# Selective scan on one core: dt replication ahead of the y products, and dt and du released step by step

## The reference, cut to what matters

```python
def step(h, inp):
    u_t, dt_t, B_t, C_t = inp
    dA = jnp.exp(jnp.clip(dt_t[..., None] * A, -20.0, 0.0))
    dB_u = jnp.clip(dt_t[..., None] * B_t[:, None, :] * u_t[..., None], -10.0, 10.0)
    h = jnp.clip(h * dA + dB_u, -100.0, 100.0)
    y = jnp.einsum('bds,bs->bd', h, C_t)
    return (h, y)
h0 = jnp.zeros((Bsz, d_inner, d_state), u.dtype)
_, ys = jax.lax.scan(step, h0, xs)      # one step for each of the T tokens
```

## Time and profile before

| | |
|---|---|
| median of three runs | 6533.08 us |
| profiled execution, its own time | 6532.31 us |
| its span, first to last instruction | 6530.6 us |
| the scan's part of it (first dt matmul at 4350.1, last y product at 5867.7) | 1517.6 us |
| VectorE busy over the span | 4930.3 us (75%) |
| ScalarE busy over the span | 3779.0 us (58%) |

### The profile page before, as it was taken

How to read it: one execution, slowest core, us unless ns; L and a number is a source line. 1 busy time by engine, 2 the same in 40 slices (tenths; PEclk the granted TensorE clock), 3 DMA queues, 4 the chain that set the end, 5 groups by cost and what they waited for, 6 DMA issues and landing times. The chain is left out here.

```text
span 6530.6 us, 93690 instructions
## 1 busy us (share of the span) xinstructions
PE 5225.0 (80%) x27420; PEld 2029.7 (31%) x27420; DVE 4930.3 (75%) x10471; ACT 3779.0 (58%) x5329; POOL 1363.7 (21%) x1658
## 2 busy tenths in 40 slices
PE   6979799797979799795999644438888888877778
PEld 3333333333333333333666322201111111115555
DVE  6666675767666675766888698879999999986768
ACT  4555555555555555552444466657777777774433
POOL 0000000000000000000111244443333333334421
PEclk8989899897989899897999866655555555558999
DMA  0000000000000000001111133331111111115422
GB/s 23 1 14 1 14 1 1 14 1 14 1 14 1 14 1 1 7 1 38 42 41 42 61 117 117 111 106 44 45 45 45 44 44 45 45 39 161 156 90 71
DMA packets 198904, 273.56 MB, mean 42 GB/s; under 512 B 13989, under 2 KB 157989, under 8 KB 192454
## 3 DMA queue, kind: packets, MB, share of 16 engines
q1 hardware_dynamic: 181190, 252.90, 12.7%
q10 hardware_dynamic: 17408, 16.78, 0.7%
HBM read 151.14 MB, written 118.49 MB: 41 GB/s over the span
## 5 line engine op out<-in xcount | busy, mean ns | idle before, releaser
L644 DVE TENSOR_REDUCE at_nmax<-at_ps_t 128x1 f32<-128x512 f32 x2048 | 1321.1, 686 | 584.4 <-PE at_ps_t L344 567.1
L486 ACT ACTIVATE at_probsT<-at_ps_s 128x1024 f32<-128x1024 f32 x1024 | 1046.0, 1023 | 810.3 <-PE at_ps_s L369 810.3
L2045 DVE SCALAR_TENSOR_TENSOR sc_decayed<-sc_da,sc_state 128x256 f32<-128x256 f32 x2048 | 777.3, 425 | 141.5 <-ACT sc_da L2000 141.5
L2000 ACT ACTIVATE sc_da<-sc_da,sc_a_col 128x1024 f32<-128x1024 f32 x512 | 560.0, 1094 | 346.2 <-PE sc_da L1936 346.2
L2055 DVE CUSTOM_DVE_ANT_0 sc_state<-sc_xd,sc_decayed 128x256 f32<-128x256 f32 x2048 | 757.3, 410 | 0.0
L344 PE MATMUL at_ps_t<-at_qkT 108*128 108x512 bf16 x2048 | 711.5, 413 | 42.8 <-DVE at_nmax L644 19.4
L1912 POOL TENSOR_SCALAR sc_xd<-sc_xd 128x1024 f32<-128x1024 f32 x512 | 533.1, 1041 | 957.4 <-ACT sc_xd L2007 957.4
L1948 PE MATMUL sc_ps_du<-sc_parts,sc_sel 24*128 24x512 bf16 x1024 | 565.4, 609 | 203.5 <-ACT sc_xd L2007 203.5
L2007 ACT ACTIVATE sc_xd<-sc_ps_du,sc_bt 128x512 f32<-128x512 f32 x1024 | 651.8, 696 | 5.9 <-PE sc_ps_du L1948 5.9
L378 PE MATMUL at_ps_o<-at_probsT,at_v 128*32 128x256 f32 x8192 | 633.2, 392 | 1.2
L365 PE MATMUL at_ps_s<-at_qkT 108*128 108x512 bf16 x2048 | 624.0, 387 | 0.0
(11 more groups left out here) (308 smaller groups left out, 7983.5 us busy)
## 6 DMA issues: line engine op xcount, KB each, us to landing
dt_parts<-si_pt SPq DMA_DIRECT2D x64, 384.0 KB, 2.6
du_parts<-si_pu SPq DMA_DIRECT2D x64, 384.0 KB, 3.2
sc_parts<-dt_parts SPq DMA_DIRECT2D x128, 192.0 KB
sc_parts<-du_parts SPq DMA_DIRECT2D x128, 192.0 KB
u_tok<-si_ut SPq DMA_DIRECT2D x8, 2048.0 KB, 8.3
y<-sc_yo SPq DMA_DIRECT2D x256, 64.0 KB
so_yin<-y SPq DMA_DIRECT2D x32, 512.0 KB
so_uin<-u_tok SPq DMA_DIRECT2D x32, 512.0 KB
```

Source lines behind the costliest of these rows:

```text
L486: nc.scalar.activation(probsT[:, c % RING, :], ps_s[c % 2][:], ACT.Exp).then_inc(s_exp, 1)
L644: nc.vector.tensor_reduce(nmax[:, par, c, t:t + 1], ps_t[c][:], AX_X, ALU.max, negate=True).then_inc(s_max, 1)
L2000: nc.scalar.activation(flat, flat, ACT.Exp, scale=a_col[:]).then_inc(s_da, 1)
L2045: nc.vector.scalar_tensor_tensor(decayed[:, ch], da[q % 2][:, j % 2, ch], DECAY_MIN, state[:, (j - 1) % SRING, ch], ALU.max, ALU.mult).the ...
```

## The change

It has four parts. In TensorE's turn dt of pair q + 2 now stands ahead of the y products of the last round, where it stood behind them. Each dt matmul waits only for its own step of the pair that held the buffer before, instead of both waiting for the whole pair. Each dt and du matmul counts its semaphore up by one, where only the second of a pair did. And ScalarE's `inputs` waits before each of its two copies for that step's du, where it waited once for both. `decays` still waits for both steps, and SyncE waits for the same matmuls under the new count.

```diff
--- before.py
+++ after.py
@@ -1855,8 +1855,8 @@
             def turn(it, g, first, last):
                 for h in range(2):
                     if not last:
-                        sp.wait_ge(s_rdt, it * NPAIR + h * HP + HP)
-                        sp.wait_ge(s_rdu, it * NPAIR + h * HP + HP)
+                        sp.wait_ge(s_rdt, it * STEPS + (h + 1) * TL)
+                        sp.wait_ge(s_rdu, it * STEPS + (h + 1) * TL)
                         load(it + 1, h)
                     if h == 0 and not first:
                         store(it - 1, 1 - g)
@@ -1930,12 +1930,11 @@
                 h = q // HP
                 if q % HP == 0:
                     pe.wait_ge(s_in[h][0], 16 * it + 16)
-                if not first:
-                    pe.wait_ge(s_dec, (n - 1) * 2 * NC)
                 for j in range(2):
-                    last = nc.tensor.matmul(da[q % 2][:, j], sel[0:KR, :], parts[0:KR, h, q % HP * 2 + j],
-                                            start=True, stop=True)
-                last.then_inc(s_rdt, 1)
+                    if not first:
+                        pe.wait_ge(s_dec, ((n - LEAD) * 2 + j + 1) * NC)
+                    nc.tensor.matmul(da[q % 2][:, j], sel[0:KR, :], parts[0:KR, h, q % HP * 2 + j],
+                                     start=True, stop=True).then_inc(s_rdt, 1)
 
             def replicate_du(it, q, first=False):
                 n = it * NPAIR + q
@@ -1945,9 +1944,9 @@
                 for j in range(2):
                     if not (first and q == 0):
                         pe.wait_ge(s_xd, 2 * n - 1 + j)
-                    last = nc.tensor.matmul(ps_du[:, j * HALF:(j + 1) * HALF], sel[Q1:Q1 + KR, :],
-                                            parts[Q1:Q1 + KR, h, q % HP * 2 + j], start=True, stop=True)
-                last.then_inc(s_rdu, 1)
+                    nc.tensor.matmul(ps_du[:, j * HALF:(j + 1) * HALF], sel[Q1:Q1 + KR, :],
+                                     parts[Q1:Q1 + KR, h, q % HP * 2 + j], start=True, stop=True
+                                     ).then_inc(s_rdu, 1)
 
             def add_y(it, g, r):
                 if r == 0:
@@ -1962,14 +1961,14 @@
 
             def turn(it, g, first, last):
                 for q in range(NPAIR):
+                    if q + LEAD < NPAIR:
+                        replicate_dt(it, q + LEAD)
+                    elif not last:
+                        replicate_dt(it + 1, q + LEAD - NPAIR)
                     if q % 2 == 0 and q > 0:
                         add_y(it, g, q // 2 - 1)
                     elif q == 0 and not first:
                         add_y(it - 1, 1 - g, ROUNDS - 1)
-                    if q + LEAD < NPAIR:
-                        replicate_dt(it, q + LEAD)
-                    elif not last:
-                        replicate_dt(it + 1, q + LEAD - NPAIR)
                     if q + LEAD + 1 < NPAIR:
                         replicate_du(it, q + LEAD + 1)
                     elif not last:
@@ -1995,15 +1994,15 @@
                 nc.scalar.copy(yo[:, g], ps_y[:]).then_inc(s_yo, 1)
 
             def decays(n, q):
-                act.wait_ge(s_rdt, n + 1)
+                act.wait_ge(s_rdt, 2 * n + 2)
                 flat = da[q % 2][:].rearrange("p j d -> p (j d)")
                 nc.scalar.activation(flat, flat, ACT.Exp, scale=a_col[:]).then_inc(s_da, 1)
 
             def inputs(n, q, fresh=False):
-                act.wait_ge(s_rdu, n + 1)
                 if not fresh:
                     act.wait_ge(s_state, (n - RING + 1) * 2 * NC)
                 for j in range(2):
+                    act.wait_ge(s_rdu, 2 * n + j + 1)
                     nc.scalar.activation(xd[:, q % RING, j], ps_du[:, j * HALF:(j + 1) * HALF], ACT.Copy,
                                          scale=bt[:, bass.ds(2 * n + j, 1)]).then_inc(s_xd, 1)
```

## The result

The changed kernel takes 6372.98 us, the median of four runs (6370.21 to 6377.51), against 6532.95 before: a ratio of 0.9755, 95% interval 0.9738 to 0.9772. The forecast was 6380, with a range of 6368 to 6445. A second measurement of the same kernel, further down, gave 6378.38 and 0.9764 (0.9751 to 0.9778).

What follows compares the result with a forecast made beforehand. A TensorE and ScalarE loop of 5.79 us a round was taken to keep VectorE waiting for exp; freed, VectorE's 1.327 us steps give a 1357.8 us scan, 153 less, so 6380 us with a range of 6368 to 6445.

Steps and rivals of the forecast that it cites:

- The loop y, dt, `decays`, `inputs`, du: In the scan before the change, TensorE and ScalarE without VectorE: 5.79 us a round, 6.29 once in an iteration.
- 1023 steps of 1.327 and a half: VectorE's `decayed` starts in the scan, if it never waits: 1357.8 us where it was 1511.2, so 153 us go.
- The loop without `decays`: TensorE and ScalarE after the change, through y, du, `inputs` and dt: 4.81 to 5.24 us a round, below VectorE's 5.31.
- The even pairs: `decays` of pair q + 2 done 3.91 us after pair q's first VectorE step, wanted at 5.31: 1.4 to spare.
- The copy of the y bank: ScalarE's copy once an iteration, 4.65 us after D, pair q's first VectorE step: costs nothing, or 0.1 if late.
- Counts by steps: Four more dt and du matmuls a round count up: taken as 0, at most 0.10 us a matmul.
- The clip, the loads, the ring of states: GpSimd's clip and SyncE's loads cost nothing; waits for clip or state ring have margins of 1.0 and 1.3 us.
- the chain: From dt through y, du, `inputs` and `decays` to odd pair q + 3: done 7.45, wanted 7.96, 0.51 us spare.
- TensorE as the bound: First rival: dt and du matmuls no longer overlap, 5.40 us a round against 5.31, 6403 or 6430 us; chance 0.13.
- Dearer handovers: Second rival: the odd pairs' chain is x longer than its margin, a round grows x/2, 6406 to 6444; chance 0.12.
- Stopped overlap: Third rival: waits in TensorE's queue stop overlap and loading weights ahead, 6.20 us a round, 6605 us; chance 0.05.
- Another wait of VectorE: Fourth rival: VectorE finds an equally long wait, the clip or the ring of states, so 6532 us; chance 0.06.

## Why the prediction was right

**The bound.** The loop y, dt, `decays`, `inputs`, du was read rightly, and so was what takes its place. The term that carries the forecast, 1023 steps of 1.327 and a half, gave 1357.8 us and was measured at 1357.8, in four profiles: the changed kernel twice, and twice with an added copy. What the forecast missed is not in the scan: the span lost 159.5 us, the scan 153.4. The other 6.1 lie before it (4.6, its start) and behind it (1.5), and the second run of the same code has its start later than the kernel before had. So I take the 7 us beyond the forecast for the spread of the other phases, and no further gain is to be explained. That the term came out to the digit is partly luck. Nearly all steps of the changed kernel are 1.325; eight of about 1.53, one in every 128 steps and at the same steps in both profiles, and a few slightly longer ones make the mean 1.327. The prediction's rows had 1.327 for another reason: steps behind a short wait. It is 2 us of the scan; what the eight pauses are was not looked for.

**Terms that were mis-sized.** A handover from a du matmul to `inputs` is 0.73, not the 0.67 of dt to `decays`, so the shortest margin is 0.43 (0.37 in one round of eight), not 0.51. The 0.03 us from the end of `decays` to VectorE's start had no term; it takes that much of the margin. The loop without `decays` was put at 4.81 to 5.24 and is 4.97. The even pairs were said to have 1.4 us: 5007.14 to 5008.07 are 0.93. I had `decays` follow dt at 2.82 and forgot that `inputs` of the same pair stands ahead of it in ScalarE's list until 3.26. None of this reached the end. The copy of the y bank cost nothing, as said: it waits for y (27.5 us in all) and starts 4.75 behind D instead of 4.65, but `inputs` behind it starts 5.27 from its D, as in other rounds.

**Costs put at nothing.** Counts by steps: shown at nothing twice, in kernels where TensorE's loop sets the time, and the added waits once. In the changed kernel itself such a cost would be hidden in the margins. The clip, the loads, the ring of states: no wait of VectorE in the list. The order of the two waits in `inputs` was overlooked; it is worth 0.08 us of handover and 11 us where the chain binds. In the changed kernel it would fit in the margin of 0.43 (an estimate; it was not run).

**The rivals.** TensorE as the bound: not so, it waits for `decayed` and runs du beside dt. Dearer handovers: true by 0.06, inside the margin. Stopped overlap: du and dt still start 0.01 apart. Another wait of VectorE: none in the list; the eight pauses of 0.2 us come to under 2 us.

**What the change's parts do.** The order without the rest takes 78 us out of the scan. The rest without the order takes out nothing. Together they take out 153, since the release by steps and the waits' order bring the bounds that the order of the work leaves, the chain at 5.57 and the loop at 5.48, below VectorE's 5.30. Within the release by steps that of du matters more than that of dt.

## What to carry to other kernels

Find the loop that sets a steady round by adding up distances between starts until they close on the round itself, and then do the same for every loop that is left once the change is made, the engine with the recurrence included: the largest gives the new round. A chain that serves only every second unit counts by half, and rounds of two lengths that alternate are its sign: add up both. Read each distance in the kernel in question; a handover that was 0.73 in one kernel was 0.84 in its neighbour. An edit that measures at nothing alone may be what keeps the second bound below the first, so parts are to be tried on top of each other, not only alone. Put the wait that is expected to end last directly ahead of the instruction.

## What the runs showed of the hardware

A count on each matmul delayed no matmul behind it by anything to be measured: 768 more in the critical loop are 0.4 us. ScalarE starts 0.84 us behind the matmul it waits for if another wait stands between, 0.76 if not. VectorE starts 0.03 us after the end of the `decays` it waits for. And TensorE's list showed 0.39 us more once in eight rounds, in two kernels where it had no time to spare; that this is the loop's jump back is argued from the place.
